# Calling a recurrence's own pieces due three steps early in a planner that writes the order of five engines

## The reference

```python
xr, gate = jnp.split(x @ W_in.T, 2, axis=-1)
xc = silu(conv(xr + t_emb))                      # causal, 4 taps, by channel
xn = layernorm(xc) * ln_g + ln_b
Bm, Cm, dt = jnp.split(xn @ W_xproj.T, 3, axis=-1)
...
def step(h, inputs):                             # h: 8 x 16 x 1024
    h = jnp.clip(h * ad[:, :, None] + bd[:, :, None] * xt[:, None, :], -10.0, 10.0)
    return h, jnp.einsum('bd,bdh->bh', ct, h)
...
y = ys + D * xn
out = x + (y * silu(gate)) @ W_out.T
```

## Time and profile before

| | |
|---|---|
| median of 3 runs | 6607.86 us |
| profiled execution | 6600.43 us, span 6598.6 us |
| first step of the recurrence starts | 3532.6 us into the span |
| last step starts | 6480.6 us |
| TensorE / VectorE / ScalarE / GpSimd busy | 92% / 69% / 36% / 49% |
| mean granted clock of TensorE | 0.96 |

### The profile page before, as it was taken

The page is one execution under the profiler, slowest core; times in us unless marked ns, Lnnn a source line. Parts: engine busy times, 40 slices in busy tenths (PEclk is TensorE's granted clock), DMA queues, the critical chain, the costliest instruction groups (busy, mean ns, idle before and its releaser), DMA issues. The chain is left out here.

```text
span 6598.6 us, 73169 instructions
## 1 busy us (share of the span) xinstructions
PE 6050.3 (92%) x24000; PEld 2755.6 (42%) x24000; DVE 4564.2 (69%) x5830; ACT 2347.9 (36%) x4460; POOL 3207.4 (49%) x2625
## 2 busy tenths in 40 slices
PE   7999999999999999999986779998999989899997
PEld 3444444444444444444343324444443434444343
DVE  4655656556555555565546988889898888889882
ACT  2444434435344343444453323233232323233110
POOL 1775766667567675675742323324142333414212
PEclk8999999999999999999988899999999999999998
DMA  2222222232232322313223344434344443434433
GB/s 88 79 83 85 89 62 89 75 96 81 68 92 63 103 74 74 92 57 92 75 67 102 82 109 112 120 89 136 83 124 108 111 124 98 126 87 124 110 90 99
DMA packets 411564, 613.29 MB, mean 93 GB/s; under 512 B 58768, under 2 KB 189968, under 8 KB 410672
## 3 DMA queue, kind: packets, MB, share of 16 engines
q1 hardware_dynamic: 374320, 558.24, 30.4%
q10 hardware_dynamic: 36864, 50.38, 3.0%
HBM read 305.31 MB, written 201.38 MB: 77 GB/s over the span
## 5 line engine op out<-in xcount | busy, mean ns | idle before, releaser
L1125 POOL TENSOR_TENSOR acc<-acc,prob 128x512 f32<-128x512 f32 x1536 | 1908.3, 1279 | 963.3 <-PE bank L815 741.5
L1055 DVE TENSOR_REDUCE mx<-bank 128x1 f32<-128x512 f32 x2048 | 1314.9, 684 | 589.3 <-PE bank L785 584.5
L2064 DVE SCALAR_TENSOR_TENSOR g<-xps,bd,g 128x1024 f32<-128x1024 f32 x1024 | 1312.9, 1282 | 244.3 <-PE xps L1794 168.4
L948 ACT ACTIVATE prob<-misc 128x512 f32<-128x512 f32 x1496 | 842.9, 597 | 853.8 <-PE misc L802 690.5
L1794 PE MATMUL xps<-sx,spread 128*128 128x512 f32 x2048 | 891.8, 522 | 244.4 <-DVE g L2064 230.3
L785 PE MATMUL bank<-khat,qhat 96*128 96x512 f32 x2048 | 990.1, 534 | 39.2 <-DVE mx L1055 20.3
L2070 DVE TENSOR_SCALAR g<-g,lim 128x1024 f32<-128x1024 f32 x1024 | 872.7, 852 | 31.1
L802 PE MATMUL misc<-qhat,khat 98*128 98x512 f32 x1679 | 723.8, 461 | 59.2 <-ACT prob L948 42.8
L1794 PEld LDWEIGHTS xps<-sx,spread 128*128 128x128 f32 x2048 | 355.4, 195 | 775.9 <-DVE g L2064 463.8
L1808 PE MATMUL yps<-g,cexp 128*32 128x512 f32 x4096 | 612.6, 636 | 0.1
L785 PEld LDWEIGHTS bank<-khat,qhat 96*128 96x128 f32 x2048 | 391.2, 196 | 433.2 <-issue 299.9
(11 more groups left out here) (211 smaller groups left out, 6845.7 us busy)
## 6 DMA issues: line engine op xcount, KB each, us to landing
sx<-scratch_xhl SPq DMA_DIRECT2D x512, 128.0 KB, 5.0
scratch_dx<-dx SPq DMA_DIRECT2D x64, 512.0 KB, 2.7
scratch_xhl<-xhi SPq DMA_DIRECT2D x64, 512.0 KB, 4.0
scratch_xhl<-xn SPq DMA_DIRECT2D x64, 512.0 KB, 4.8
scratch_y<-ysb SPq DMA_DIRECT2D x512, 64.0 KB
dx_t<-scratch_dx SPq DMA_DIRECT2D x59, 512.0 KB, 6.3
y_t<-scratch_y SPq DMA_DIRECT2D x59, 512.0 KB, 3.7
xt_n<-in_x SPq DMA_DIRECT2D x112, 256.0 KB, 2.9
```

Of the source, the lines that this page charges most:

```text
L948: act.activation(to, bank[m][:, 0:QC], ACT.Exp, scale=SCALE).then_inc(sem[f"act_m{m}"], 1)
L1055: dve.tensor_reduce(self.mx2[:, h * TT + qt, c:c + 1], bank[m][:, 0:QC], AX.X, ALU.max).then_inc(sem[f"dve_m{m}"], 1)
L1125: pool.tensor_tensor(self.acc[:, a, h, :], self.acc[:, a, h, :], self.prob[:, (n % 2) * GH + h, :], ALU.add).then_inc(sem["pool_acc"], 1)
L2064: dve.scalar_tensor_tensor(self.g[:, t % 4, :], self.xps[t % 2][:, :], self.bd[:, i % 2, tl:tl + 1], self.g[:, (t - 1) % 4, :], ALU.mult, ...
```

## The change

Two numbers of the planner. Every piece of the recurrence's lane (`steps`) gets a due step that is 3 smaller, and in the last chunk (i = 7) the lane `finish(6, ...)` has its due steps spread over 1 to 125 of the chunk's 128 steps in place of 1 to 129. No instruction is added or removed, and no tile, wait rule or duration is changed; the orders on all five engines are written anew.

```diff
         def put(t, engine, took, piece, after, signals, **k):
             out.append(item(engine, took, piece, after, signals, **k))
-            out[-1]["due"] = t
+            out[-1]["due"] = t - 3.0
...
         if i:
-            order.lane(finish(i - 1, SIDE, 0, range(B)), t + 1.0, t + TOK + 1.0)
+            order.lane(finish(i - 1, SIDE, 0, range(B)), t + 1.0, t + TOK + (1.0 if i < NCH - 1 else -3.0))
```

## The result

The changed kernel takes 6454.77 us in the median of four runs (6452.40 to 6457.49), the kernel before 6604.98 us beside it: a ratio of 0.9776, with an interval of 0.9758 to 0.9794. That is 150 us less. I had forecast 63 us less, and the range ended at 6505. The profiled execution took 6452.4 us, its span is 6450.6 us, 148.0 shorter than before.

A forecast was written before the change was run, and what follows sets the result against it. PE and DVE were taken to wait for each other in turn in the middle chunks, PE alone to bound chunk 7. Terms -53 + 6 - 6 - 5 + 0 + 8 - 13 + 0 = -63 took 6607.9 to 6545 us; range 6505 to 6595.

The forecast's parts named there:

- The first third: Steps 0 to 31 of the six middle chunks: side-matmul blocks ahead of `x` are cut up, -53 us.
- the wait of step 4: Early in chunk 3, `q(388)` starts after 4.55 us of DVE idleness; forecast gone in every middle chunk.
- the place of the 4.55 us: Chunk 3, `x(388)` behind `xr`, `out` and two `gm`; the wait was to fall to some 0.2 us.
- The middle: Steps 32 to 78 of the six middle chunks: waits stay, larger blocks add 1 us a chunk, +6 us.
- `pjo` waits for `pj` ... 0: DVE's 58.0 us of waits in 33 places: pairs stand as close together as before, so no change.
- The low-clock rival: In the middle chunks PE idles ahead of two side-work bulks, each then at half rate: 6643 us, chance 0.08.
- The last third: Steps 79 to 127 of the six middle chunks: half of 11 us of waits goes, -6 us.
- Chunk 7: Last chunk, bound by PE alone: only its 10 us of idle time can be saved, -5 us.
- Chunk 0: First chunk: `q` idled 14.6 us for `x` there; the forecast had no separate term for it.
- The port: DVE instructions held up by GpSimd on the shared port: up to 16 more meetings, +8 us.
- The tail: After the last step: freed bank, fewer leftover `om`, idle stretches and slow groups, -13 us.

The follow-up runs named there:

- The fillers: Two unused 128x512 matmuls ahead of the `x` before the first `pj` of a half chunk, added to the kernel before: 6566.94 us, ratio 0.9934.

## Why the prediction was wrong in size, step by step

- **The first third, -53.** Measured -67 over six chunks. Right in mechanism and place: the blocks are cut up, and the wait of step 4 is gone in chunks 2 to 6, where it had been 4.0 to 5.3 us (chunk 1 had none). Over the six chunks `q` waits there for `x` 13.5 us in place of 63.7, 50 us less for the 53 that I took off. (In the working for the place of the 4.55 us I held `q(389)` against the moment at which DVE asks for `q(388)`; it is wanted a step later, so that no wait was to be left.) What I missed is that DVE's side work is held back too: 3.4 us of it left this third of chunk 3 for the middle, and 21 over the six chunks. So some of this gain is only moved, and the middle's is larger by it than its -41 shows.
- **The middle, "I leave that and add 1 us a chunk, +6": this is the step that failed**, and with it "`pjo` waits for `pj` ... 0". Measured -41, outside my bounds of -10 and +25. The waits that I left standing there fell, those for `x` from 33.0 to 14.1 us (my share of 41, scaled up from chunk 3, was too large as well) and those for `pj` from 36.6 to 2.4. I read from the order at one place that the blocks grow, and costed what a larger block delays; over the whole part the waits for `x` became shorter all the same. And I did not ask what PE does when it has no block. Before, side matmuls were done as soon as they were due, so PE had none in stock where DVE was away for bn statistics; in chunk 3 it idled 1.97 us, fell to the 1.2 GHz level, and ran `pj`, which DVE then waits for, at half rate. Side work held back up to 3 steps fills that time. The fillers show what this cost: with the order unchanged they win 4.7 us a chunk, some 29 of the 41. The other 12 are the shorter waits for `x`, less the work moved in; what in the new order makes them shorter was not tried.
- **The low-clock rival had a mechanism that is real and the wrong sign for the middle.** I argued that a PE that does `x` first idles ahead of its bulks. It is the reverse there at 3 steps: a stock of ready work keeps PE from idling (its waits for `q` fell by 66 us in the recurrence), and time at the low clock fell from 79 to 29 us in the middle part. In the last third it rose from 34 to 80 us, so that the mean clock of chunks 1 to 6 is 0.97 as before. At 24 steps the clock does fall, to 0.94, and the kernel is slower than before. The Trainium skill ("TensorE: Matmul & The Clock Gate", section "HAM oscillation — how this bites in real kernels") describes idling between groups of matmuls that makes the next group slow; the traces agree with that (behind 1.97 us of idle time 3.48 us for 1.88 in `pj`). I had applied it to the changed order alone and not to the order of before, where the earlier trace rows and a clock of 0.97 already showed that it happens.
- **The last third, -6.** Measured +5. The waits for `x`, of which I took half off, did not change (18.7 us over the six chunks before, 18.0 now; my share of 11 was too small). With TensorE's pieces alone early the third takes 120.4 us and not 126.6, and these waits are 3.6 us; so the early due steps of the rest of the lane, most likely of `q` and `g`, cost there. I had looked at DVE's ties only for the port.
- **Chunk 7, -5:** measured -8.6, inside its bounds. **Chunk 0, 0:** -9.5. It takes 348.8, 353.1 and 351.9 us in the three traces with the old ties, 339.3 and 338.9 in the two with the changed kernel's, and 339 to 346 where other pieces or steps up to 6 are early; what makes it shorter was not tried and stays open.
- **The port, +8.** Four more meetings (84 to 88) are some 4 us at 1.0 us each. The longest `g` is 1920 ns, 1.1 us over the median, again less than a GpSimd instruction of 1.28 us.
- **The tail, -13.** Measured -25.5. I had worked out the floor, 66 us of work in 91.2, and then took only half of the difference off; the changed kernel stands on that floor (65.4). With the bank free no idle time is left between groups, and of the slow groups one is left, the first.

The steps sum up so: -67 - 41 + 5 in the middle chunks, -8.6, -9.5, -25.5 and -1.4 for the start make -148. Against my -63, the middle accounts for 47 of the missing 85 us, the first third for 14, the tail for 13, chunk 0 for 10, the port's 8 (which lie within the parts) and chunk 7 and the start for 5; the last third takes 11 back.

## What to carry to other kernels

Where two engines pass a serial chain to and fro, let the chain's pieces win ties on the engine that also has bulk work, but only by a few steps: a small stock of ready side work fills that engine's gaps and can keep its clock up, a large one starves whoever waits for the side work, so try several sizes, and try the chain's two engines apart: here TensorE's pieces alone did best. When costing such a change, ask of the old order too what its idle stretches do to the matmuls behind them. Work that is left over at a change of phase and holds a buffer of the new phase, here an open accumulation in a bank, is best finished first; and if the work of the new phase has a floor, cost the tail by that floor.

## What the runs showed of the hardware that I had not expected

- More matmuls made the kernel faster: 32 records that nothing reads, four in each of eight places and 1.88 us there, took the median from 6603.71 to 6566.94 (0.9934 [0.9916, 0.9951]), some 5 us a place. In chunk 3 they stood ahead of a `pj` whose sixteen records then took 1.88 in place of 3.48 us.
- An idle stretch as short as 1.54 us or 1.97 us, behind a few microseconds in which PE had only transposes, `x` and an `out`, was followed by half rate (an `om` in 1.7 us for 0.86 to 0.89, `x` in 1.22 for 0.73), while 1.84 us of idleness behind a busy stretch was not: the eight records of `xr` that follow took 3.70 us.
- The idle time of PE does not foretell the clock by itself: in the last third of the six middle chunks PE waited 62.5 us for `q` in the changed kernel and 78.3 us before, and yet spent 80 us at the low clock in place of 34. The changed kernel spends 181 us of its recurrence at the low clock, the one with TensorE's pieces alone early 102, at 6454.77 and 6441.54 us; whether the clock is what separates them, or the order on DVE that goes with it, was not tried apart.
